# A Mamba recurrence on one core: GpSimd drives five states instead of six in every second sequence

## What is computed

```
x_dbl = u @ W_x.T
dt = softplus(x_dbl[..., :4] @ W_dt.T + b_dt)
Bs, Cs = x_dbl[..., 4:20], x_dbl[..., 20:]
A = -exp(A_log)
def step(h, (dt_t, B_t, C_t, u_t)):
    h = exp(dt_t[..., None] * A) * h + (dt_t * u_t)[..., None] * B_t[:, None, :]
    return h, einsum('bdn,bn->bd', h, C_t)
y = ys + u * D_skip
out = y * silu(z) @ W_out.T
```

## Time and profile before

| | us |
|---|---|
| median of 3 runs | 719.66 (719.37 to 720.05) |
| the profiled execution, its own time | 722.11 |
| its span in the trace | 720.3 |
| busy PE / DVE / POOL / ACT | 619.4 / 570.9 / 452.1 / 422.0 |
| POOL: hc products x128 / dbu products x48 | 299.4 / 113.8 |
| DVE: scans x128 / products with dtu x80 | 291.8 / 97.2 |

### The profile page before, as it was taken

One profiled execution on the slowest core, in us unless ns is written; L12 is line 12 of the kernel. 1 busy time (PEld: TensorE's weight loads), 2 busy tenths in 40 slices (PEclk: granted clock), 3 DMA queues, 4 the chain that ended last, 5 costly groups with the idle time before them and its releaser, 6 DMA issues.

```text
span 720.3 us, 10778 instructions
## 1 busy us (share of the span) xinstructions
PE 619.4 (86%) x3697; PEld 266.3 (37%) x3726; DVE 570.9 (79%) x578; ACT 422.0 (59%) x655; POOL 452.1 (63%) x240
## 2 busy tenths in 40 slices
PE   8978888779878878977888787988889978999997
PEld 3322222213212222222222222355656335777762
DVE  4799899999999999999999998355554545666645
ACT  4689678577568567665765753443545424555532
POOL 7599989999999999999999999500001300000002
PEclk9989999999999999999999999999999999999999
DMA  3866569686666665666676762000000000000001
GB/s 102 238 226 223 207 218 282 234 271 217 223 231 237 225 253 206 234 215 229 225 253 215 249 208 85 1 1 1 2 12 2 1 18 2 1 2 1 3 1 63
DMA packets 32105, 101.17 MB, mean 140 GB/s; under 512 B 6821, under 2 KB 7342, under 8 KB 32046
## 3 DMA queue, kind: packets, MB, share of 16 engines
q1 hardware_dynamic: 30806, 99.48, 41.2%
q10 hardware_dynamic: 920, 0.81, 0.4%
q0 software_dynamic: 320, 0.13, 0.1%
HBM read 94.64 MB, written 2.10 MB: 134 GB/s over the span
## 4 chain that ended last, share of the span: by engine, by line
PE 42%; DVE 22%; issue 20%; ACT 10%; POOL 3%; DMA 2%; DVEq 1%; SPq 0%; ACTq 0%; POOLq 0%
DVE hh_all L1559 9%; DVE pb L1554 7%; PE py L229 7%; PE pb L198 6%; PE px L252 5%; PE py L748 4%; POOL hc L1868 2%; PE pb L973 2%; ACT da L1255 2%; PE px L777 2%; PE pb L736 2%; ACT px L1194 1%; PE px L695 1%; PE px L242 1%; DVE dtu_all L1533 1%
## 5 line engine op out<-in xcount | busy, mean ns | idle before, releaser
L1868 POOL TENSOR_TENSOR hc<-hh_all,cc 128x1024 f32<-128x1024 f32 x128 | 299.4, 2369 | 8.4 <-DVE hh_all L1559 7.6
L1559 DVE TENSOR_TENSOR_SCAN hh_all<-da,pb 128x1024 f32<-128x1024 f32 x80 | 182.9, 2287 | 5.2 <-ACT da L1255 2.0
L748 PE MATMUL py<-hc,w_cst 64*64 64x512 f32 x1024 | 151.5, 653 | 9.7 <-DVE yg L1570 9.7
L1882 POOL TENSOR_TENSOR yg<-w_xs 128x512 f32<-128x512 f32 x10 | 12.6, 1266 | 234.5 <-DVE w_xs L1693 143.0
L1879 POOL TENSOR_TENSOR dbu<-bb,dtu_all 128x1024 f32<-128x1024 f32 x48 | 113.8, 2371 | 3.2 <-DVE dtu_all L1533 3.2
L1559 DVE TENSOR_TENSOR_SCAN hh_all<-pb,dbu 128x1024 f32<-128x1024 f32 x48 | 108.9, 2269 | 1.7 <-DVE dtu_all L1533 1.7
L1554 DVE TENSOR_TENSOR pb<-pb,dtu_all 128x1024 f32<-128x1024 f32 x80 | 97.2, 1215 | 2.3 <-PE pb L736 0.3
L736 PE MATMUL pb<-bc,w_sel 128*128 128x512 bf16 x137 | 47.7, 420 | 56.1 <-DVE hh_all L1559 53.8
L1255 ACT ACTIVATE pb<-dt_all,w_aneg 128x1024 f32<-128x1024 f32 x48 | 53.6, 1116 | 66.2 <-DVE hh_all L1559 65.8
L1255 ACT ACTIVATE da<-dt_all,w_aneg 128x1024 f32<-128x1024 f32 x80 | 89.8, 1138 | 2.2 <-DVE dt_all L1540 1.4
L286 DVE TENSOR_REDUCE gate_all<-pb 128x1 f32<-128x1024 f32 (+7 forms) x64 | 60.4, 986 | 30.8 <-PE pb L208 16.1
(11 more groups left out here) (302 smaller groups left out, 957.7 us busy)
## 6 DMA issues: line engine op xcount, KB each, us to landing
cc<-scr SPq DMA_DIRECT2D x128, 512.0 KB, 4.3
bb<-scr SPq DMA_DIRECT2D x48, 512.0 KB, 5.0
w_xs<-w_xm SPq DMA_DIRECT2D x8, 256.0 KB, 6.7
w_xs<-hc SPq DMA_DIRECT2D x6, 256.0 KB, 3.9
scr<-bcf SPq DMA_DIRECT2D x8, 128.0 KB, 4.6
out<-yg SPq DMA_DIRECT2D x4, 256.0 KB, 3.0
w_xst<-in_x SPq DMA_DIRECT2D x1, 512.0 KB, 4.4
w_cst<-in_consts ACTq DMA_DIRECT2D x1, 404.0 KB, 5.4
```

Source lines behind the costliest of these rows:

```text
L748: last = nc.tensor.matmul(py[part(t), half(r)], ident[part(r), part(r)], hc[u % NHC][part(r), half(t)], start=(n == 0), stop=(n == NS - 1) ...
L1559: nc.vector.tensor_tensor_scan(hh[u % NHH][:, :], decay[:, :], drive[:, :], 0.0, ALU.mult, ALU.add).then_inc(scan_done, 1)
L1868: nc.gpsimd.tensor_tensor(hc[u % NHC][:, :], hh[u % NHH][:, :], cc[u % NCC][:, :], ALU.mult).then_inc(hc_done, 1)
```

## The change

Sequences 0, 2, 4 and 6 keep the tuple. Sequences 1, 3, 5 and 7 get `(1, 4, 8, 11, 14)`: 44 pooled units instead of 48, and 84 own ones instead of 80. The counting functions and the waits that used `NP` now count pooled units one by one; their values in the even sequences mean the same units as before. The file becomes one line shorter, so every later line number is less by one.

```
-        POOLED = (1, 4, 7, 9, 12, 14)
-        NP = len(POOLED)
+        POOLED = [((1, 4, 7, 9, 12, 14), (1, 4, 8, 11, 14))[q % 2] for q in range(NSEQ)]
...
         def pooled(u):
-            return u % NS in POOLED
+            return u % NS in POOLED[u // NS]
 
         def pool_count(u):
-            return NP * (u // NS) + sum(1 for n in POOLED if n < u % NS)
+            return sum(1 for v in range(u) if pooled(v))
...
             if s >= 2:
-                dve.wait_ge(pooled_done, NP * (s - 1))
+                dve.wait_ge(pooled_done, pool_count(NS * (s - 1)))
...
-                for i in range(2 if NP else 0):
-                    sp.wait_ge(bb_in[i], 16 * ((NP * (s - 1) + 1 - i) // 2))
+                for i in range(2):
+                    sp.wait_ge(bb_in[i], 16 * ((pool_count(NS * (s - 1)) + 1 - i) // 2))
```

More of the change, by code:

```diff
@@ L404, in build_all @@
         cc = [sb(f"cc_{i}", [DI, L]) for i in range(NCC)]
-        bb = [sb(f"bb_{i}", [DI, L]) for i in range(2 if NP else 0)]
-        dbu = [sb(f"dbu_{i}", [DI, L]) for i in range(NDB if NP else 0)]
+        bb = [sb(f"bb_{i}", [DI, L]) for i in range(2)]
+        dbu = [sb(f"dbu_{i}", [DI, L]) for i in range(NDB)]
         ex, rl = sb("ex", [DI, L]), sb("rl", [DI, L])
```

## The result

The changed kernel takes **727.36 us** (median of 4 runs, 726.77 to 728.95) where the kernel before takes 719.86 us beside it (4 runs, 719.37 to 721.69): a ratio of 1.0098, 95% interval 1.0079 to 1.0118. That is +7.5 us. The forecast was +3.7 us (723.3 us), the range ended at 726.3 us, so the sign was right and the size was not. The profiled execution of the change took 727.38 us (span 725.5 us), right on its median. That of the kernel before took 722.11 us, 2.25 us above its own, so the two traces differ by only 5.2 us in span.

A forecast was written before the change was run, and what follows sets the result against it. The prediction took VectorE to set the pace, with GpSimd following closely. Its terms, 4.96 - 1.00 - 0.27 = +3.7 us, took the median from 719.66 to 723.3 us, range 720.9 to 726.3 us.

The forecast's parts named there:

- Step 1: GpSimd, odd sequences: one drive product fewer in each, 9.3 us of work, worth 0 because VectorE's own work hides it.
- The rival in which GpSimd sets the pace: Recurrence: GpSimd, not VectorE, limits it, so its relief makes the run faster, about 718.1 us; chance 0.08.
- Step 2: VectorE, odd sequences: one added product of 1.24 us in each of four counts in full, +4.96 us.
- Step 3: Sequences 1, 3, 5: the scan of state 11 no longer waits for its decay from ScalarE, -1.00 us.
- Step 4: VectorE, behind the second work on dtu: a product follows where a pooled scan did, 3 x 0.09 = -0.27 us.
- steps 5 and 6: Odd sequences: TensorE's added B row stays hidden by 1.4 us or more and GpSimd's drives come in time; both worth 0.
- The first rival: Odd sequences: the state 11 wait stays and the state 12 row comes late, +4.7 to +6.7 us; chance 0.18.
- Step 7: End of the last sequence: lighter GpSimd starts the attention no earlier, and VectorE's 1.24 us come through in full.
- the sign of being wrong: Odd sequences: the forecast is wrong if one costs less than 0.5 us or more than 1.6 us.
- The sum: Whole run: 4.96 - 1.00 - 0.27 = +3.7 us, the median going from 719.66 to 723.3 us.
- a possible gain behind the recurrence: Attention: TensorE's clock might fall better there, part of the no-visible-change case, less than 1.4 us from 719.66; chance 0.08.
- the new wait in odd sequences: The first rival by its title: waits for state 11 and the state 12 row, at most 726.4 us; chance 0.18.

The follow-up runs named there:

- e7: Kernel before, with GpSimd's drive of state 9 in the odd sequences made for only half the columns: 720.63 us, gap 0.0 us.
- e10: Changed kernel with matmuls of zeros in each of TensorE's idle places in the recurrence: 725.35 us, ratio 1.005 to the kernel before.
- e9: Kernel before, order unchanged, with matmuls of zeros wherever TensorE idles over 1.5 us for a scan in the recurrence: 718.07 us, ratio 0.997.
- e2: Kernel before with five GpSimd states at the new positions in sequence 7 only: 724.89 us, +3.6 us over the kernel before.
- e3: Changed kernel with matmuls of zeros at state 13 of sequences 2, 4, 6 and the last: 724.99 us, ratio 1.0058 to the kernel before.
- e11: Changed kernel with 16 matmuls of zeros at state 13 of the last sequence alone: 724.64 us, ratio 1.0067 to the kernel before.
- e1: Kernel before with five GpSimd states at the new positions in sequences 1, 3 and 5 only: 723.78 us, ratio 1.0052.
- e4: Kernel before with matmuls of zeros at state 13 of sequences 2, 4, 6 and the last: 720.52 us, ratio 0.9994.
- e8: Kernel before, with VectorE's product of state 10 in the odd sequences made for only half the columns: 721.24 us, gap +0.6 us.
- e5: The changed kernel as it is, timed again beside the kernel before: 727.64 us, ratio 1.0096.

## Why the prediction was wrong, point by point

*Step 1, GpSimd's relief is worth 0*: right as far as e7 goes, which takes away half a drive. The rival in which GpSimd sets the pace had this change end at 718.1 us; it took 727.36 us. The Trainium skill (Perfetto Trace Analysis, section Identifying the Most-Contended Engine) would have the engine of highest occupancy relieved first. The measurement says otherwise here: GpSimd had the higher occupancy (99.5% of the middle, VectorE 97.6%), and its relief bought nothing (e7, 0.0 us).

*Step 2, +4.96 us*: right. With TensorE kept at full clock the four odd stretches are 4.79 us longer (e10 against e9), which is steps 2 and 4 together (4.96 - 0.27 = 4.69 us) within 0.1 us.

*Step 3, -1.00 us*: right for the pair of traces, and its reason holds: the decay of state 11 was late because TensorE ran the row of state 8 and what follows at 1.2 GHz. But e9 removes the same waits without any change of order. The saving was one that the lower clock had made possible, and I booked it as the order's own.

*Step 4, -0.27 us, and steps 5 and 6*: right. No product of state 12 or 9 waited for its row in an odd sequence, and no scan for GpSimd. The first rival named the lower clock, but in the odd sequences and for the row of state 12; that its time (725 to 726.4 us) came nearest of all is luck.

*Step 7, "DVE's 1.24 us come through in full"*: **this is the step that failed.** The end gave +3.73 us where it said 1.24, beyond the 1.6 us that it had named as the sign of being wrong. 1.24 of them are the product, and that part stands (e10 against e9: +1.27 us); 2.21 are the lower clock on sixteen sums ahead of the q and k projection (gone in e2, e3, e10 and e11, whose last sequence has the same order); 0.28 I did not locate. I looked there for GpSimd's last product and not for TensorE's, although the attention starts behind TensorE.

*The sum*, "the added operations take as long in either": the even sequences were costed at nothing. But with the odd sequences changed, the lower clock fell ahead of an output product with a B row behind it in sequence 4, +1.5 us (e1 has the same 53.08 us). That the moved steps of VectorE bring this about, by moving TensorE's idle times, is argued. I took the clock as a possible gain behind the recurrence and, in the first rival, as a loss in the odd sequences, but never as a loss in the even ones or at the end, with the earlier trace rows showing a row of 1.03 us instead of 0.61 before my eyes. The two places together are 1.49 + 2.49 us (all of stretch 7 but 1.24) = +4.0 us, the start gave 2.3 back in the traces, and odd stretches plus 1.24 make the +3.7 forecast: 3.7 + 4.0 - 2.3 - 0.6 (stretches 2 and 6) + 0.4 (behind) = 5.2 us, the difference of the spans. The range ended at 726.3 us because its upper end knew only the new wait in odd sequences.

The remaining 2.25 us between 5.2 and the 7.5 of the medians are the profiled execution of the kernel before, slow by that against its own median. Its lower clock at 80 us would account for 1.65 of them if most of the other executions did not have it. Traces of e4, e7 and e8 have the same slow start, but so has that of e5, an execution right on the median of the changed kernel. Which of the other executions had it was not recorded, so this stays argued. Open too is why the changed kernel is slow in all 11 executions (the two traced ones have the lower clock in the same two places), while e3, e10 and e11, which differ by some added matmuls, reach from 719 to 729 us, and why e10 and e9 are 7.3 us apart as whole runs. What is shown is the split inside the recurrence. From the first to the last gated output it is 364.08 and 364.05 us in the two traces of the changed kernel, and 356.97 in that of the kernel before (356.81 in e4, 356.98 in e7): +7.1 us, about as much as the medians differ, and made of the order and of two late rows at the lower clock.

## What to carry to other kernels

In a trace like this one, in which TensorE idles 2 us at a time for a slower engine, the matmul durations depended on the execution and on the order. So before costing an edit, list the rows that run at the lower clock and who waits behind each, and give the rows that have no slack (a product between two needed rows, the last sums ahead of the next stage) both durations. A term that comes from such a row belongs to the clock, not to the edit. And filling TensorE's idle time with products of zeros into an open sum is cheap to try: it was worth 0.3% on the kernel before, with nothing else changed. It is no cure for a spread of executions: e10 still reaches from 719.01 to 727.19 us.

## What the runs showed of the hardware that was not expected

The clock fell after idle times of TensorE of only 2 to 3 us each, between matmuls (1.97 us ahead of 285.21, 2.14 us ahead of 441.07, 3.0 us ahead of the row of state 8). The Trainium skill (TensorE: Matmul & The Clock Gate, section HAM oscillation — how this bites in real kernels) describes a kernel that falls back to the lower clock at each wait between bursts and pays for it each time. This trace agrees, with a difference in what is paid: 16 sums at 3.69 us instead of 1.95, but a cost in time only where somebody waits for them (0 for the v projection of e2, 1.7 to 2.2 us at the last sums).

One kernel's executions differ by up to 10 us (e3, 719.23 to 729.35) with the mean granted clock between 0.972 and 0.956, so that one profile of such a kernel is one draw, and a median of three another. GpSimd has next to no room left beside the faster VectorE of e9: over the six sequences from 95.0 to 400.2 us it makes 132 products and waits for a scan once, 1.0 us.
